# Transposed attention scores for four heads at once in the two rotary layers of a four-layer decoder

## The reference

```python
q, k = rope(x_norm @ Wq.T), rope(ctx @ Wk.T)        # rotated by cos and sin of the position
s = (q @ k.T) / sqrt(128)                           # 128 x 128 per head and sequence
s = where(mask, s, very_negative)                   # layer 2: a given mask of keys; layer 3: causal
p = softmax(s)
x = x + tanh(gate) * ((p @ v) @ Wo.T)
```

## Time and profile before

| | us |
|---|---|
| median of 3 runs | 2085.89 |
| lowest and highest run | 2085.34, 2087.68 |
| span of the profiled execution, first to last instruction | 2084.6 |

### The profile page before, as it was taken

One profiled execution on the slowest core, in us unless ns is written; L12 is line 12 of the kernel. 1 busy time (PEld: TensorE's weight loads), 2 busy tenths in 40 slices (PEclk: granted clock), 3 DMA queues, 4 the chain that ended last, 5 costly groups with the idle time before them and its releaser, 6 DMA issues.

```text
span 2084.6 us, 28881 instructions
## 1 busy us (share of the span) xinstructions
PE 1921.0 (92%) x9672; PEld 1540.9 (74%) x9672; DVE 1348.5 (65%) x2451; ACT 806.1 (39%) x2324; POOL 1016.7 (49%) x816
## 2 busy tenths in 40 slices
PE   5999999988877999999999998779999999999987
PEld 3777777776456878778778786658787887878866
DVE  5444444475675776767777767757767777677675
ACT  3444444340412444443443434124434434434441
POOL 2122222245246665665655755156656557556551
PEclk9999999997778999999999999989999999999999
DMA  4000000011001110110110101011101001001001
GB/s 165 20 20 19 19 19 20 19 45 45 32 6 31 51 36 15 50 35 15 50 30 20 55 21 34 0 31 51 36 15 50 29 21 49 26 25 50 26 6 41
DMA packets 37772, 69.34 MB, mean 33 GB/s; under 512 B 4522, under 2 KB 8362, under 8 KB 37586
## 3 DMA queue, kind: packets, MB, share of 16 engines
q1 hardware_dynamic: 37714, 68.62, 10.9%
HBM read 66.50 MB, written 2.10 MB: 33 GB/s over the span
## 4 chain that ended last, share of the span: by engine, by line
issue 33%; POOL 26%; PE 21%; DVE 14%; ACT 5%; POOLq 0%; DMA 0%; SPq 0%; DVEq 0%
POOL rope_a L1314 7%; PE ps L337 7%; PE ps L338 6%; PE ps L339 6%; POOL q_loL L1326 5%; POOL wq_loL L1292 5%; POOL probs L1331 4%; POOL wo_loL L1292 3%; ACT ot_hi L1122 2%; DVE rope_b L800 1%; DVE rope_b L799 1%; DVE rope_a L798 1%; DVE stats L724 1%; POOL wkv_loL L1292 1%; DVE xn L737 1%
## 5 line engine op out<-in xcount | busy, mean ns | idle before, releaser
L1314 POOL TENSOR_TENSOR rope_a<-rope_a,rope_b 128x512 f32<-128x512 f32 x160 | 208.1, 1300 | 383.1 <-DVE rope_b L800 383.1
L1331 POOL TENSOR_TENSOR probs<-probs,rsums 128x512 f32<-128x512 f32 (+1 forms) x160 | 193.9, 1212 | 367.0 <-DVE rsums L822 367.0
L1110 ACT ACTIVATE probs<-ps,nbias 128x128 f32<-128x128 f32 (+1 forms) x640 | 239.9, 388 | 190.9 <-DVE nbias L818 190.9
L337 PE MATMUL ps<-wo_hiL,ot_hi 128*128 128x512 f32 (+1 forms) x640 | 265.7, 415 | 15.8 <-POOL wo_loL L1292 8.7
L337 PE MATMUL ps<-xt_hi,wq_hiL 128*128 128x512 f32 (+1 forms) x640 | 256.1, 400 | 1.4 <-DVE v_loL L769 0.8
L338 PE MATMUL ps<-wo_loL,ot_hi 128*128 128x512 f32 (+1 forms) x640 | 252.6, 395 | 0.0
L339 PE MATMUL ps<-wo_hiL,ot_lo 128*128 128x512 f32 (+1 forms) x640 | 252.4, 394 | 0.0
L339 PE MATMUL ps<-xt_hi,wq_loL 128*128 128x512 f32 (+1 forms) x640 | 251.7, 393 | 0.0
L338 PE MATMUL ps<-xt_lo,wq_hiL 128*128 128x512 f32 (+1 forms) x640 | 251.4, 393 | 0.0
L831 DVE TENSOR_TENSOR ot_lo<-ps,ot_hi 128x512 fp32r<-128x512 f32 (+1 forms) x160 | 110.5, 690 | 180.8 <-ACT ot_hi L1122 180.8
L1118 ACT CAST pt_hiL<-ps 128x512 fp32r<-128x512 f32 (+1 forms) x160 | 107.3, 671 | 251.2 <-PE ps L501 251.2
(11 more groups left out here) (204 smaller groups left out, 4541.7 us busy)
## 6 DMA issues: line engine op xcount, KB each, us to landing
raw<-in_L_proj SPq DMA_DIRECT2D x96, 256.0 KB, 2.6
raw<-in_L_out SPq DMA_DIRECT2D x64, 256.0 KB, 2.6
raw<-in_L_proj SPq DMA_DIRECT2D x24, 192.0 KB, 2.4
raw<-in_F_w SPq DMA_DIRECT2D x16, 256.0 KB, 2.7
raw<-in_L_out SPq DMA_DIRECT2D x16, 192.0 KB, 2.4
x<-in_x SPq DMA_DIRECT2D x8, 256.0 KB, 4.0
ct_raw<-in_ctx_t SPq DMA_DIRECT2D x4, 512.0 KB, 7.2
cn_raw<-in_ctx SPq DMA_DIRECT2D x8, 256.0 KB, 8.5
```

What stands on the lines that cost most here:

```text
L337: pe.matmul(dst, l_hi, r_hi, start=start, stop=False)
L1110: e = act.activation(probs[:, at_:at_ + L.keys], ps[:, bank + at_ // 512, at_ % 512:at_ % 512 + L.keys], ACT.Exp, bias=nbias[:, b % 2, h:h ...
L1314: gp.tensor_tensor(rope_a[:, a], rope_a[:, a], rope_b[:], ALU.add).then_inc(L.s_rsum, 1)
L1331: gp.tensor_tensor(pv, pv, rsums[:, b % 2].unsqueeze(2).to_broadcast([P, GH, L.keys]), ALU.mult).then_inc(L.s_p, 1)
```

## The change

Scores are formed transposed: the keys of one sequence are stationary, and the queries of all four heads pass as 512 columns (`keys_queries`, three products into the new bank 5). DVE adds a mask of 0 or -2^100 while it copies them from PSUM to a new SBUF tile `st` (`masked`). `scores` is now four PE transposes of `st` into the score bank. The softmax scale goes into the cos and sin tables on both sides, so the masking in place (L812) and the scaling of the maximum (L818) go, and the exponentials take the maximum itself. `st` exists once: `masked(b + 1)` waits for `scores(b)`, and `keys_queries(b + 1)` waits for `masked(b)`.

```diff
+                def keys_queries(b, i, ahead=0):
+                    if b or ahead:
+                        pe.wait_ge(L.s_st, B * i + B * ahead + b)
+                    if b % HALF == 0:
+                        pe.wait_ge(L.s_qk, L.ready("KQ", i, b // HALF) + ahead * L.kinds_group("KQ"))
+                    tok = slice(b * P, (b + 1) * P)
+                    out = ps[:, ST_BANK, :].rearrange("p (h t) -> p h t", h=GH)
+                    triple(pe, out, L.k_hi[:, b, 0], L.k_lo[:, b, 0], L.q_hi[:, :, tok], L.q_lo[:, :, tok],
+                           True, True).then_inc(L.s_kq, 1)
...
                 def scores(b, i):
                     pe.wait_ge(L.s_e, B * i + b + 1)
+                    if L.rope:
+                        pe.wait_ge(L.s_st, B * i + b + 1)
+                        for h in range(GH):
+                            mm = pe.transpose(ps[:, bank, h * P:(h + 1) * P], st[:, h * P:(h + 1) * P], ident)
+                        mm.then_inc(L.s_s, 1)
+                        return
...
                         if b >= 1:
                             heads_out(b - 1, i)
+                        if L.rope and b < B - 1:
+                            keys_queries(b + 1, i)
...
                     heads_out(B - 1, i)
+                    if L.rope and not last:
+                        keys_queries(0, i, 1)
                     if not last:
                         fillers(B - 1, i, only=1)
...
+                if L.rope:
+                    keys_queries(0, 0)
                 with pe.Fori(0, L.groups - 1) as i:
...
                 def row_max(b, i):
                     v.wait_ge(L.s_s, B * i + b + 1)
+                    v.tensor_reduce(negmax[:, b % 2], sc, X_AXIS, ALU.max, negate=True).then_inc(L.s_smax, 1)
                     if L.rope:
-                        v.sem_inc(L.s_seen, 1)
-                        v.copy_predicated(sc, m.to_broadcast([P, GH, P]), ...)
-                    v.tensor_reduce(negmax[:, b % 2], sc, X_AXIS, ALU.max, negate=True).then_inc(L.s_smax, 1)
+                        return
                     v.tensor_scalar(nbias[:, b % 2], negmax[:, b % 2], L.scale, None, ALU.mult).then_inc(L.s_nb, 1)
+
+                def masked(b, i, ahead=0):
+                    v.wait_ge(L.s_kq, B * i + B * ahead + b + 1)
+                    if b or ahead:
+                        v.wait_ge(L.s_s, B * i + B * ahead + b)
+                    v.tensor_tensor(st[:].rearrange("p (h t) -> p h t", h=GH),
+                                    ps[:, ST_BANK, :].rearrange("p (h t) -> p h t", h=GH),
+                                    m.to_broadcast([P, GH, P]), ALU.add).then_inc(L.s_st, 1)
...
                             ot_tail(b - 1, i)
+                        if L.rope and b < B - 1:
+                            masked(b + 1, i)
...
+    each = P ** -0.25
+    cos = (_np.concatenate([_np.cos(ang), _np.cos(ang)], 1) * each).astype(f)
```

More of the change, by code:

```diff
@@ L35 @@
 LN_EPS = 1e-5
+MASKED = -2.0 ** 100
 FILL_ROPE = {3: [("K", 0), ("Q", 0)], 4: [("Q", 1), ("W", 0)], 5: [("V", 0), ("Q", 2)], 6: [("Q", 3)]}
@@ L161, in build @@
         minus_half = new("minus_half", [P, 1], F32)
-        fill = new("fill", [P, 2], F32)
         negmax = new("negmax", [P, 2, GH], F32)
         nbias = new("nbias", [P, 2, GH], F32)
+        st = new("st", [P, GH * P], F32)
         sums = new("sums", [P, 2, GH], F32)
@@ L196, in build @@
         rot3 = at("rot3", [P, 2, P], F32, r_k + 8192)
-        mask2 = at("mask2", [P, B, P], U8, r_v + 8192)
-        mask3 = at("mask3", [P, 1, P], U8, r_v + 8192 + 1024)
-        causal = at("causal", [P, P], F32, r_v + 8192 + 1280)
+        mask2 = at("mask2", [P, B, P], F32, r_v + 8192)
+        mask3 = at("mask3", [P, 1, P], F32, r_k + 8192 + 1024)
         mask_in = at("mask_in", [P, B, P], I32, r_v)
@@ L418, in _ @@
             sp.dma_start(rot3[:], inp["rope3"]).then_inc(rot3_in, 16)
+            sp.dma_start(mask3[:, 0], inp["causal"]).then_inc(rot3_in, 16)
             attention(Lq[2])
@@ L864, in group @@
                     ot_tail(B - 1, i)
+                    if L.rope and not last:
+                        masked(0, i, 1)
                     if not last and not L.rope:
@@ L878, in attention @@
                         evacuate(b, k, 0, PROLOGUE)
+                if L.rope:
+                    masked(0, 0)
                 with v.Fori(0, L.groups - 1) as i:
@@ L1042, in _ @@
             feed_forward(1)
-            v.wait_ge(m_in, 32)
-            v.tensor_scalar(mask2[:], mask_in[:], 0.0, None, ALU.is_equal)
-            v.tensor_scalar(mask3[:, 0], causal[:], 0.0, None, ALU.is_equal).then_inc(m_done, 1)
+            v.wait_ge(m_in, 16)
+            v.tensor_scalar(mask2[:], mask_in[:], 0.0, MASKED, ALU.is_equal, ALU.mult).then_inc(m_done, 1)
             v.wait_ge(m_done, 1)
@@ L1048, in _ @@
             feed_forward(2)
-            v.wait_ge(rot3_in, 16)
+            v.wait_ge(rot3_in, 32)
             attention(Lq[2], "A3")
@@ L1106, in exps @@
                     bank = S_BANK + (b % 2 if L.sources == 1 else 0)
[L1107 removed]
+                    act.wait_ge(L.s_smax if L.rope else L.s_nb, B * i + b + 1)
+                    offset = negmax if L.rope else nbias
                     for h in range(GH):
@@ L1473, in shape_constants @@
     ang = (_np.arange(C * P, dtype=f)[:, None] * inv[None, :]).astype(f)
-    cos = _np.concatenate([_np.cos(ang), _np.cos(ang)], 1).astype(f)
-    sin = _np.concatenate([-_np.sin(ang), _np.sin(ang)], 1).astype(f)
+    each = P ** -0.25
+    cos = (_np.concatenate([_np.cos(ang), _np.cos(ang)], 1) * each).astype(f)
+    sin = (_np.concatenate([-_np.sin(ang), _np.sin(ang)], 1) * each).astype(f)
     rope2 = _np.stack([cos, sin], 1).reshape(C, P, 2, P).transpose(1, 0, 2, 3)
@@ L1486, in shape_constants @@
     fourier = four.astype(f).reshape(C, P, n).transpose(1, 0, 2)
-    causal = _np.tril(_np.ones((P, P), f))
+    causal = _np.where(_np.arange(P)[:, None] <= _np.arange(P)[None, :], 0.0, MASKED).astype(f)
     row = 8 * _np.arange(B)[None, :, None] + (_np.arange(P) // 16)[:, None, None]
@@ L1517 @@
     arr["pos"] = a["pos_BxS2"].reshape(1, T)
-    arr["mask"] = a["mask_BxSxS2_ik0"].transpose(1, 0, 2)
+    arr["mask"] = a["mask_BxSxS2_ik0"].transpose(2, 0, 1)
     arr["gates"] = _np.stack([a["g_xattn"], a["g_ffn"]], 1).reshape(1, 8)
```

28 lines of the change are left out of this document (9 added, 19 removed).

## The result

The changed kernel takes 2135.56 us (median of 4 runs, 2134.57 to 2137.89), the one before 2085.98 (4 runs beside it): a ratio of 1.024, 95% interval 1.023 to 1.0256. The change makes the kernel 2.4% slower, 49.6 us. The forecast was 26 us; its direction and its mechanism came out, its size did not, and the time lies 5.6 us above the top of the range.

What follows compares the result with a forecast made beforehand. PE, busy 92% of the span, was taken as the bound. 2084.6 + 6 (passes) + 4 (prologue) - 2 (last groups) + 18 (clock) = 2110.6 us; with the median 1.3 higher 2112 us, 1.2% slower; range 2088 to 2130.

Steps and rivals of the forecast that it cites:

- the clock: PE at half clock after each group's new idle: 1.3 us a group, +18 in all; bounds 0 and 3.4 a group.
- the structure of the passes: Steps of a rotary loop pass summed to 80.5 us against 80.02: +0.4 a group, +6 over 14 groups.
- the last groups: Last group of each rotary layer: Q3 taken up earlier, stall 1.1 us, shorter chains; -1 a layer, -2 in all.
- The prologue's +4: Before each rotary layer's first scores: masked(0) stands behind the last rotation, transposes(0) start +1.9 us later a layer.
- The wait moved, step 3: keys_queries(4) waits for Q3's low part ahead of both fillers: PE idles 3.7 us, step 3 lasts 14.2 us, before 11.44.
- S: The start of scores(3) in step 3; Q3's low part was predicted to end at S + 8.0.
- rival C: Clock stays down twice as long, or a second step waits (masked copy 1.76 us): 2130 us and up; chance 0.09.
- A: Stall at keys_queries(4) short, PE's relief wins: 2068 us with half the stall, 2042 with none; chance 0.14.
- B: Stall at keys_queries(4) as computed, but no slow clock: 2094 us; chance 0.14.

Runs made afterwards that it cites:

- the run with the stall filled: Changed kernel with 13 unused products of 512 columns put into PE's idle ahead of keys_queries(4): 2109.31 us, ratio 1.0114.
- the two runs that leave the stall alone: Changed kernel with masked(0) ahead of the prologue's last rotation (2126.69 us); changed kernel with keys_queries and masked copy reordered except in step 3 (2097.00 us).
- the wait behind the fillers: Changed kernel with keys_queries(4) behind both fillers of step 3 and masked(4) behind the K tile's rotation on DVE: 2059.80 us, ratio 0.988.
- the prologue alone: Changed kernel with one line moved, masked(0) ahead of the prologue's last rotation: 2126.69 us, ratio 1.0205.
- the order alone: Changed kernel with keys_queries ahead of heads_out and masked copy ahead of ot_lo in all steps but step 3: 2097.00 us, ratio 1.0056.

## Why the prediction was wrong in size and right in kind

**The steps that failed.** The sum had 26 of the trace's 48.1 us. The missing 22 are three terms: the clock, put at +18 and measured at +26; the structure of the passes, +6 and +15; the last groups, -2 and +2.6. The prologue's +4 came out as a number and not as a cause.

**The wait moved, step 3: right.** The idle at keys_queries(4) was put at 3.7 us and came out at 3.49 in every pass, S + 8.0 at S + 8.03. Taking the chain's rows of before and shifting them by the work removed ahead of it worked, because DVE, ACT and POOL do the same work in the same order between pt_lo and q_lo as before, POOL's normalisation between its sum and its low part included.

**The clock: right in kind, the term too small.** 1.3 us a pass was taken, 18 in all; the run with the stall filled shows 26. One stretch of 3.4 us costs 1.5 to 1.6 us (half of it, less a little), where 1.3 allowed for a part that falls into the idle or on a wait. Of the short stretches at most 0.2 us lay in the idle, of the long ones 0.7 to 0.9; the rest fell on products, because behind the stall PE has fillers enough for any stretch. And four passes behind the first of a layer had a stretch twice as long, at 2.75 us each. These four and the eight short ones make 23 us, the two first passes 3. The end of the bound, 3.4 us if the clock stays down twice as long, was written down and then given to rival C as an all-or-nothing case; it came in five passes of 14, as a mixture. The Trainium skill (TensorE: Matmul & The Clock Gate, "What's actually happening") has the half clock as the default, which activity lifts. The runs bear this out for an idle of 3.49 us, 14 times of 14 in the change and 40 of 42 with the two runs that leave the stall alone; taken as "every stall is punished", which is how the prediction read it, it is too strong: with 2.15 us it held 7 times of 14.

**The structure of a pass: +0.4 taken, +1.07 measured.** With the clock held, steps 0 and 1 are 13.34 us (13.3 predicted), step 2 8.36 (8.2), step 3 14.37 (14.2), steps 4 and 5 19.2 (19.1), steps 6 and 7 25.84 (25.7). Each estimate is short by 0.04 to 0.17. None is a mistake of mechanism, but all lean the same way: 0.6 us a pass, 9 us over 14 with the first passes. The likely reason, argued and not shown, is that every handover between engines was put at nothing. A sum of small differences between large steps needs the error of a step times their number in its range, and the range did not have it.

**Last groups: -1 a layer taken, +1.28 measured.** The stall of 1.1 there was 0.84. What was missed is that scores(4) to scores(7) each wait 0.9 to 1.4 us for a masked copy, scores(5) longest with 1.41. DVE's timeline there:

```profile
1282.99 0.69 DVE L857 TENSOR_TENSOR ot_lo<-ps,ot_hi 128x512 fp32r<-128x512 f32 x1 [0.47 <-ACT ot_hi L1152]
1283.59 0.68 DVE L842 TENSOR_TENSOR st<-ps,mask 128x512 f32<-128x512 f32 x1
```

The copy stands behind ot_lo, and with no fillers on PE nothing covers that. The prediction had seen this chain for steps 2 and 6 and did not carry it to the last group, where every step has it. With the copy ahead of ot_lo and keys_queries ahead of heads_out layer 2's last group is 2.9 us shorter, so this order is the reason; which of the two moves counts for more is open.

**Prologue: right place, no clock term.** Counted from the first product of the prologue's last tile, scores(0) start 4.5 us later than before, and the forecast had 4.3. But transposes(0), put at +1.9, start 4.9 us later in layer 2 and 3.6 in layer 3: behind the idle of 3.57 us the clock is half for 6.8 us in the one (from 664.3 us on) and for 3.4 us in the other. The clock term was given to the loops and not to the prologue. The sum of the trace hides this. It shows +4.1 for the prologues and everything outside the groups, though scores(0) alone come twice 4.5 us later, because 3.2 us came back ahead of layer 2's prologue and 1.8 behind the last group; whether the conversions of the masks that went are the cause was not tried. That +4 was predicted and +4.1 measured is chance.

**The rivals.** A, a short stall and PE's relief winning, did not come. The relief is there, though: with the wait behind the fillers the kernel runs at 2060 us, where A gave 2042 with no stall. 3.3 us a pass were credited to everything but the stall, and it gave 2.2. B, no slow clock, fell in all passes; made by hand it gives 2109 instead of the 2094 predicted, by the shortfalls above. The forecast's point for B that idles at the very start show no fall was misread: in the trace of before the products from 34.9 to 39.2 us, behind an idle of 9.65, start 0.43 us apart, as at half clock, and from 41.5 us on 0.23 apart, though the granted clock reads 1.00 all along. C's time, 2130 us and up, is where the measurement lies; its mechanism came in part, the long stretch in five passes of 14, and its masked copy of 1.76 us not at all (0.69).

**The chances** put 0.82 on slower, and the range's top was set where rival C began. With the two ends that were on paper, the clock to 3.4 a pass and the structure's errors all one way, it would have reached past 2140.

## What to carry to other kernels

When a change puts a product into an earlier step, look not at how long the product takes but at which chain must be done before it and what stands behind it in the queue: one call moved behind two others was worth 76 us here. On PE count an idle of over 2 us with the slow clock that may follow it, at every place where one arises, the prologue included, and price the long stretch as well as the short one. And when a kernel is faster with useless products in a stall than without, the stall's place is what to mend, not its length.

## What the runs showed of the hardware

**Like idles, unlike slow stretches.** Fourteen idles of 3.49 us, at full clock before and followed by the same products, led to 3.4 us at half clock nine times and to 6.8 us five times. Idles of 2.15 us led to none or to 3.4 us, seven times each. Nothing in the kernel differs between these passes, but the traces show a difference in time. With the prologue alone and with the order alone the idle of 3.49 us comes 28 times more. Of the 42 idles in all, 13 led to the long stretch, and in each of these the clock fell 0.65 us or more before the idle ended; 27 led to the short one, and there it fell 0.6 us before the idle's end or later, up to 1.5 us behind it; two led to none. The moment of the fall was only read off and not set by any run, so what decides it is open.

**The conditional copy was long only behind a running POOL operation.** COPY_PREDICATED took 0.70 us at one place of the kernel before and 1.76 at another, its mean over 128 being 1.14. Lines by form, the copy of before and the add that took its place (busy us, mean ns, idle before):

```profile
L812 DVE COPY_PREDICATED ps<-mask,fill 128x512 f32<-128x512 uint8 x128 | 145.6, 1137 | 82.3 <-PE ps L339 80.8
```

```profile
L842 DVE TENSOR_TENSOR st<-ps,mask 128x512 f32<-128x512 f32 x128 | 87.5, 684 | 26.8 <-PE ps L339 26.7
```

POOL's timeline of before around the copy that began at 770.53:

```profile
770.43 1.30 POOL L1292 TENSOR_TENSOR wkv_loL<-raw,wkv_hiL 128x512 fp32r<-128x512 f32 x1
771.68 1.77 POOL L1292 TENSOR_TENSOR wq_loL<-raw,wq_hiL 128x512 fp32r<-128x512 f32 x1
```

The copy ended at 772.29, 0.56 us behind POOL's first operation; POOL's next took 1.77 instead of 1.3. The same holds throughout the trace: all 74 copies that began while one of POOL's TENSOR_TENSOR ran ended 0.55 or 0.56 us behind that operation's end; the 32 that met no POOL operation took 0.69 or 0.70; and the 18 that began ahead of one of these operations took 0.70, and POOL's operation 1.69 to 1.79. The other four met a shorter operation (rstd) and took 0.69 or 0.70. The new copy shows none of this, and POOL's own operations are shorter with the change: wq_lo 1.30 us on average instead of 1.49. The Trainium skill (SBUF — State Buffer, "Reading the diagram") says that a VectorE operation with two inputs in SBUF and a GpSimd operation that reads SBUF shut each other out for a whole instruction. The copy of before read mask and fill from SBUF, the new one reads only the mask there, the scores from PSUM; the rows agree. Some 1.1 us of the 2.7 by which pt_lo begins sooner in step 3 (1.72 us behind scores(3) instead of 4.45) are this wait for POOL, so it works for the change. It was not tried by itself, and how much of the times above it makes is not shown.
